# GpSimd issues a group of gathers only once the group two places ahead of it has landed: a three-layer graph network on one core

## The reference

```python
msg = jnp.concatenate([h[src], h[dst]], axis=-1) @ Mw.T + Mb
s1 = jax.ops.segment_sum(msg, dst, num_segments=N)
s2 = jax.ops.segment_sum(msg * msg, dst, num_segments=N)
mx = jax.ops.segment_max(msg, dst, num_segments=N)
mn = jax.ops.segment_min(msg, dst, num_segments=N)
...
agg = jnp.concatenate([mx, mn, std, var], axis=-1)
...
u = jnp.concatenate([h, h_neigh], axis=-1) @ Uw.T + Ub
...
out = jax.nn.leaky_relu(u @ mix_w.T + mix_b, 0.01)
return out + h
```

## Time and profile before

| | |
|---|---|
| median of 3 runs | 1753.13 us (1748.63 to 1753.54) |
| profiled execution, first to last instruction | 2141.7 us |
| POOL busy | 1235.7 us, 58% |
| DVE busy | 1096.6 us, 51% |
| PE busy | 682.6 us, 32% |
| ACT busy | 455.6 us, 21% |

### The profile page before, as it was taken

One profiled execution on the slowest core, in us unless ns is written; L12 is line 12 of the kernel. 1 busy time (PEld: TensorE's weight loads), 2 busy tenths in 40 slices (PEclk: granted clock), 3 DMA queues, 4 the chain that ended last, 5 costly groups with the idle time before them and its releaser, 6 DMA issues. The chain is left out here.

```text
span 2141.7 us, 10446 instructions
## 1 busy us (share of the span) xinstructions
PE 682.6 (32%) x2156; PEld 402.8 (19%) x2156; DVE 1096.6 (51%) x2178; ACT 455.6 (21%) x1024; POOL 1235.7 (58%) x1358
## 2 busy tenths in 40 slices
PE   5611233132322470323132232362113322233265
PEld 5311121011111230112111111131101211112122
DVE  8600755464644843445464463572525664466464
ACT  0103321122111154111111111136101221112125
POOL 7673666676666127745675675406756666576504
PEclk9975666565655685566565666686556666656677
DMA  4363333333333033323332232204323333333200
GB/s 59 105 167 113 93 103 103 91 99 92 92 91 91 18 112 113 111 66 99 96 101 76 88 103 75 65 27 145 106 84 101 93 88 93 88 103 96 76 0 30
DMA packets 97107, 190.18 MB, mean 89 GB/s; under 512 B 30792, under 2 KB 56984, under 8 KB 97040
## 3 DMA queue, kind: packets, MB, share of 16 engines
q0 software_dynamic: 59968, 160.78, 26.6%
q1 hardware_dynamic: 37077, 28.77, 4.9%
HBM read 168.75 MB, written 17.75 MB: 87 GB/s over the span
## 5 line engine op out<-in xcount | busy, mean ns | idle before, releaser
L742 POOL DMA_INDIRECT G<-p_by_rank,index x774 | 734.8, 949 | 560.2 <-issue 227.8
L742 POOL DMA_INDIRECT G<-p_by_node,index x387 | 367.4, 949 | 225.0 <-issue 120.3
L921 PE MATMUL ps<-wide_ident,agg 128*128 128x128 f32 x288 | 80.3, 434 | 1209.3 <-issue 701.2
L1470 DVE TENSOR_TENSOR ps<-ps,G 128x1024 f32<-128x1024 f32 (+3 forms) x222 | 250.3, 1127 | 191.2 <-issue 78.4
L921 PEld LDWEIGHTS ps<-wide_ident,agg 128*128 128x128 f32 x288 | 51.5, 217 | 1239.5 <-issue 721.9
L936 PE MATMUL ps<-w_u_sb,aggT 128*128 128x384 f32 x576 | 284.3, 654 | 0.0
L1714 DVE SCALAR_TENSOR_TENSOR var<-tot,rdeg,msq 128x128 f32<-128x128 f32 x75 | 26.1, 348 | 426.4 <-ACT msq L1109 407.8
L936 PEld LDWEIGHTS ps<-w_u_sb,aggT 128*128 128x128 f32 x576 | 162.6, 282 | 144.7 <-issue 119.1
L1135 ACT ACTIVATE u_sb<-ps 128x128 f32<-128x128 f32 x75 | 20.7, 277 | 721.1 <-remote 509.0
L1472 DVE TENSOR_TENSOR ps<-ps,G 128x512 f32<-128x512 f32 (+3 forms) x222 | 141.6, 638 | 0.0
L1471 DVE TENSOR_TENSOR ps<-ps,G 128x512 f32<-128x512 f32 (+3 forms) x222 | 141.5, 637 | 0.0
(11 more groups left out here) (280 smaller groups left out, 1328.3 us busy)
## 6 DMA issues: line engine op xcount, KB each, us to landing
G<-p_by_rank,index POOLq DMA_INDIRECT x774
p_by_rank<-base SPq DMA_DIRECT2D x18, 512.0 KB
G<-p_by_node,index POOLq DMA_INDIRECT x387
p_by_node<-G SPq DMA_DIRECT2D x6, 514.0 KB
w_u_sb<-in_w_u SPq DMA_DIRECT2D x3, 768.0 KB
x_r<-rows_by_rank SPq DMA_DIRECT2D x1, 1600.0 KB
G<-shared_rows SPq DMA_DIRECT2D x12, 53.0 KB
windows<-src_pad SPq DMA_DIRECT2D x1, 624.8 KB, 14.1
```

The lines of the kernel that those rows point to most:

```text
L742: g.indirect_dma_start(G[:, n % R, j, 0:w], None, table, bass.IndirectOffsetOnAxis(ap=named, axis=0))\
L921: ins = nc.tensor.transpose(ps[:, 2, i * D:(i + 1) * D], agg[:, t % 2, i * D:(i + 1) * D], ident[:, :])
L1470: TT(run[:, 0:nk, :], run[:, 0:nk, :], G[:, n % R, 0:nk, 0:2 * D], ALU.add)
```

## The change

Ahead of a group's gathers GpSimd now waits until all gathers of the group two places ahead have landed. The wait starts with group 6, and is left out where the group two places ahead issues none:

```diff
@@ -737,6 +737,8 @@
                         pool.wait_ge(dve_used.sem, dve_used.at(l, n - R + 1))
                         if l == 0:
                             pool.wait_ge(rank_kept.sem, rank_kept.at(l, kept_to[n - R]))
+                    if n >= len(AHEAD) + 2 and own_slots[n - 2]:
+                        pool.wait_ge(gathered[(n - 2) % R].sem, gathered[(n - 2) % R].at(l, slot_before[n - 2]))
                     for j in range(own_slots[n]):
                         named = index[:, t + j, k0:k0 + 1] if n in AHEAD else index[:, t, k0 + j:k0 + j + 1]
                         g.indirect_dma_start(G[:, n % R, j, 0:w], None, table,
```

## The result

The changed kernel takes 1827.18 us (median of four runs, 1824.90 to 1828.36), the kernel before 1752.68 us (four runs). The ratio is 1.0419, with a 95% interval of 1.0407 to 1.0431: 74.5 us slower. The prediction was 23 us slower, in a range that ended at 1794 us, so it had the direction and not the size.

What follows compares the result with a forecast made beforehand. The prediction took GpSimd, issuing gathers 1.25 us apart, to bound the kernel. Holds of 17.0 + 3.1 = 20.1 us plus 3.4 for late landings gave 23 us on the median of 1753.13, so 1776 us, range 1751 to 1794.

Steps and rivals of the forecast that it cites:

- GpSimd at 1.25 us a gather sets the pace: Stage A: GpSimd issues gathers all the time, 1.25 us apart, 397 a layer, 496 us for a layer's gathers.
- The sum of 1742.7 us: Whole program before the change: start 110.8, gathers 1488.8, layer passages 69.2, end 73.9 us; 0.6% below the median of 1753.13.
- A satisfied wait costs nothing: Added waits on GpSimd whose gathers have already landed: taken as 0 us each, at most 0.27 us.
- The passage about an interval beyond 1.25 us: Sign in the changed profile: if all gathers' interval grows beyond 1.25 us, a satisfied wait isn't free, at 98 waits a layer.
- landing 2.4, plus wake-up 0.27: Price of a holding wait, minus GpSimd's issue meanwhile: 1.42 us with no gather between, 0.17 with one; 20.1 us in three layers.
- One landing in eight is 0.9 us later: Allowance for other transfers delaying landings at the 30 places with no or one gather between: 3.4 us more.
- upper end: All landings at 3.3 us at the places with no or one gather between: 12 x 2.32 + 18 x 1.07 = 47 us.
- the ring gives it back: Rival: GpSimd is ahead without a profile too, so ring waits absorb the holds; 1753 to 1756 us, chance 0.24.
- all landings are late: Rival: contention keeps every landing at 3.3 us, 1753 + 47 = 1800 us; chance 0.07 for over 40 us.
- Faster through SyncE: Rival: fewer gathers in flight let SyncE's shared-slot transfers through sooner, 1743 us; chance 0.04 of faster by over 0.3%.
- the wait never bites: Rival: the group two places ahead has always landed; its time is the given-back rival's, 1753 to 1756 us, without a separate chance.
- The sign that I had named for a dearer landing or wake-up: In the changed profile, POOL idle times of 0.5 us or more before groups with two or three gathers between.

## Why the prediction was wrong

**GpSimd at 1.25 us a gather sets the pace: right.** It was read against the profile's own picture, from the 388.6 us by which the profiled execution was too long, and the sixty gathers left out confirm it (1.26 us each). The sum of 1742.7 us lacks 7.4 us of the span of the trace with the wait three ahead, 1750.1. The start was too long by 2.8 us (first gather at 108.0 for 110.8) and the end is near (73.6 for 73.9). The passages between layers lacked 5.3 us, 37.4 and 37.2 for 34.6 each, and the gathers 5.2 (from first to last 498.3, 498.1 and 497.5 us, for 397 x 1.25 = 496.3). A little luck is in it: the passage is counted from the last gather's start, so 396 intervals a layer were due and not 397, and the extra 3.75 us hid part of what was missing.

**A satisfied wait costs nothing: right.** Some 290 of them cost 0.6 us. The passage about an interval beyond 1.25 us did not come to pass.

**The hold, "landing 2.4, plus wake-up 0.27": this step failed.** Start to start the clean hold is 3.5 us, not 2.67, and this is nearly half of the error. *Landing 2.4* was the moment when the last packet of the lone gather in the earlier trace rows went through. What a waiting engine sees is the semaphore, and by that the gather lands 2.8 us after its start (median of the changed kernel; 2.41 and 2.76 us for packets and semaphore of one gather above). *Wake-up 0.27* was taken from the earlier trace rows, where VectorE released GpSimd; after a landing it is 3.5 - 2.8 = 0.7 us (0.74 to 0.78 at the clean holds of the changed kernel). The same landing and wake-up with nothing between cost 2.25 us in place of 1.42, and with one gather between 1.0 in place of 0.17. Per layer that is 4 x 2.25 + 5 x 1.0 = 14.0 us where I had 6.7, and the two layers with short transfers measured 14.2 and 14.3. (The sixth place, group 111, costs nothing: group 110 had just been held, so the landing that 111 asks for was past. Holds in a row aren't independent, which I had overlooked, at a price of 0.5 us in the forecast.)

**"One landing in eight is 0.9 us later": this term failed too.** It should have been 10 us a layer and was 1.1. This is the other, slightly larger half of the error. The late landings are not thinly spread: nearly all the time they cost sits at the groups from 18 to 38, where SyncE brings one shared slot after the other, and three of the ten narrow places of a layer lie there (24, 27 and 36). Groups 27 and 36 are narrow because of it, since groups 26 and 35 are brought by SyncE alone. Where the wait holds longest is so also where landings are latest: group 27 started 6.34 us after the gather it asks for, against the 3.57 us (3.3 and 0.27) of the upper end. I had taken the share of the DMA engines in the earlier trace rows, 0.45 in mid-layer, as a sign that there was room; a mean over sixteen engines doesn't tell of the one that a gather must wait for.

Together, with the clean layers and layer 1 of the same run: 3 x 14.2 = 43 us of clean holds and 3 x 10 = 30 us of lateness make 73 us; the forecast had 20.1 and 3.4.

**The upper end, 47 us, was not a bound.** It used the 3.3 us of the setup's gathers, but with the wake-up of 0.27 and no landing later than that. With 3.57 us start to start it comes near the 43 us of the clean holds by luck: the landing was put too high and the wake-up too low. I did write that groups with three or more between pay only if a landing takes over 4.7 us, and then gave this no price. It happens: the maximum is 7.0 us, and the groups at two or more between pay 7.5 us in three layers, 17.1 when they are alone.

**The rivals.** That the ring gives it back fails with the ring waits gone from the trace (1.5 us). That all landings are late is wrong as put: the median is 2.8 us, and SyncE's transfers make some of them very late rather than all of them a little. Faster through SyncE: shortening its transfers to one row changed nothing without the waits. That the wait never bites is refuted by 73.7 us of holds.

**What the changed profile would show.** The idle time of 1.7 us before groups 27, 36, 45 and 75 was 5.4, 4.6, 2.5 and 2.6; the 0.5 before groups 20, 80 and 95 was 1.3, and before group 24 it was 4.4. The sign that I had named for a dearer landing or wake-up, 0.5 us or more before groups with two or more between, is there: 0.6 to 0.8 before groups 18, 34, 38, 63 and 85 of layer 2. The span was forecast at 2142 us, within 1%, and was 1826.5; VectorE's last sum was to come tens of microseconds after the last gather and came 3.1 after.

```profile
1755.79 0.42 DVE L1581 TENSOR_TENSOR tot<-ps,G 128x256 f32<-128x256 f32 x1
```

Both rested on every profiled execution of this program being as long as that of before. None of the nine that followed was; what lengthened the first is not known.

The Trainium skill's "DMA: Bandwidth & Descriptors" says in "Anatomy of one DMA" that the semaphore can't fire until the last byte is confirmed in the target memory. The runs agree in kind: with every group held, the last packet of a gather ended 2.41 us after its start and the last increment came at 2.76. By the 2.0 us and bytes/436e3 that the Trainium skill gives in the same section, 128 KB take an estimated 2.3 us; the measured landing of 2.8 is 0.5 us over it. The Trainium skill's "DMA: Bandwidth & Descriptors" advises in "Rules for kernel authors" to issue a DMA early and wait on its semaphore late. The runs agree: the wait three groups ahead costs nothing that can be told where the wait two ahead costs 75 us.

## What to carry to other kernels

A wait on a DMA costs from the issue to the next instruction's start, so take it from such a pair in a trace, not from the packets and not from the wake-up after another engine: here 3.5 us instead of 2.67. Count what lies between a wait and what it waits for at the narrowest places of the schedule, and ask what else is on the DMA engines just there; one more group of distance made the difference between 75 us and none. Where a profiled execution is far longer than the runs, sum the program up by the engine that never rests and test that sum with a run, as leaving gathers out did here, before trusting the trace's waits.

## What was unexpected of the hardware

A gather of 128 KB that usually lands in 2.8 us landed after 5.6 us while the mean share of the DMA engines was only 0.07 to 0.57: of the 64 increments of its group, 61 were in within 2.8 us. GpSimd goes on 0.7 us after a landing but 0.27 us after VectorE's release. And one profiled execution was 388.6 us longer than the runs, with ScalarE's instructions 1.40 us apart whatever their work and most semaphore records missing, while the nine others were within 5 us of their medians.
